# Third layer of a four-layer graph network: attention matrix and transformed rows split into rounded parts, their float32 product written as three rounded products

## The reference, cut to what matters

```python
h = jnp.maximum(_layernorm(x, axis=-1), 0.0)
Wh = jnp.einsum('bni,hoi->bhno', h, W) + bW[None, :, None, :]
e = jnp.einsum('bhno,hop->bhnp', Wh, attn)
scores = jnp.einsum('bhnp,bhmp->bhnm', e, Wh)
A_mat = jnp.tanh(jnp.where(adj[:, None, :, :], scores, 0.0))
```

## Time and profile before

| | |
|---|---|
| median of 3 runs | 2121.08 us (2115.74, 2121.08, 2121.89) |
| the profiled execution | 2115.82 us |
| its span, first to last instruction | 2113.7 us |
| mean granted TensorE clock | 0.991 |
| busy: PE (matmul) / PEld (weight load) | 2029.5 us (96%) / 1882.4 us (89%) |
| busy: DVE, ACT, POOL | 1488.5, 1001.3, 572.5 us (70%, 47%, 27%) |
| third layer's steps | about 753 to 1640 us of the span |

### The profile page before, as it was taken

The page is one execution under the profiler, slowest core; times in us unless marked ns, Lnnn a source line. Parts: engine busy times, 40 slices in busy tenths (PEclk is TensorE's granted clock), DMA queues, the critical chain, the costliest instruction groups (busy, mean ns, idle before and its releaser), DMA issues. The chain is left out here.

```text
span 2113.7 us, 52824 instructions
## 1 busy us (share of the span) xinstructions
PE 2029.5 (96%) x18448; PEld 1882.4 (89%) x18448; DVE 1488.5 (70%) x3344; ACT 1001.3 (47%) x2058; POOL 572.5 (27%) x624
## 2 busy tenths in 40 slices
PE   7999999899999799999999999999998899999997
PEld 7888888899999699999999999999998788888886
DVE  7989989677777455555555555555555699999997
ACT  6666666455555322232222322322222476767665
POOL 4444434222222011101111111011111444454443
PEclk9999999999999899999999999999999999999999
DMA  3222222532323201011111110111110112221221
GB/s 107 68 75 76 65 71 76 153 90 80 91 76 91 74 16 28 21 31 30 30 30 30 30 30 16 30 30 30 30 30 21 38 52 61 61 61 49 57 61 46
DMA packets 149370, 113.31 MB, mean 54 GB/s; under 512 B 42944, under 2 KB 148800, under 8 KB 149312
## 3 DMA queue, kind: packets, MB, share of 16 engines
q1 hardware_dynamic: 149312, 112.52, 18.8%
HBM read 78.93 MB, written 33.55 MB: 53 GB/s over the span
## 5 line engine op out<-in xcount | busy, mean ns | idle before, releaser
L254 POOL TENSOR_TENSOR ln_rstd<-ln_var_eps,minus_half 128x2 f32<-128x2 f32 x128 | 95.4, 745 | 888.1 <-DVE ln_var_eps L247 888.1
L1703 ACT ACTIVATE l_cat_hi<-banks 128x512 fp32r<-128x512 f32 x128 | 76.5, 598 | 261.3 <-PE banks L1874 261.3
L271 ACT ACTIVATE ln_h<-ln_x,ln_shift,ln_rstd 128x256 f32<-128x256 f32 x256 | 139.5, 592 | 57.5 <-DVE ln_shift L261 51.9
L162 PE MATMUL banks<-ln_hT_hi,square_w_hi 128*128 128x256 f32 x512 | 154.3, 301 | 5.0 <-DVE square_w_lo L628 3.2
L162 PE MATMUL banks<-ln_hT_hi,l_g_w_hi 128*128 128x256 f32 x512 | 148.5, 290 | 4.1 <-PEq L1972 4.1
L164 PE MATMUL banks<-ln_hT_hi,square_w_lo 128*128 128x256 f32 x512 | 145.7, 285 | 0.0
L163 PE MATMUL banks<-ln_hT_lo,square_w_hi 128*128 128x256 f32 x512 | 145.7, 284 | 0.0
L162 PE MATMUL banks<-l_cat_hi,l_aw_hi 128*128 128x256 f32 x512 | 144.2, 282 | 1.4 <-DVE l_cat_lo L1761 1.4
L164 PE MATMUL banks<-l_cat_hi,l_aw_lo 128*128 128x256 f32 x512 | 144.1, 281 | 0.0
L163 PE MATMUL banks<-l_cat_lo,l_aw_hi 128*128 128x256 f32 x512 | 143.9, 281 | 0.0
L164 PE MATMUL banks<-ln_hT_hi,l_g_w_lo 128*128 128x256 f32 x512 | 142.7, 279 | 0.0
(11 more groups left out here) (237 smaller groups left out, 6946.4 us busy)
## 6 DMA issues: line engine op xcount, KB each, us to landing
hidden<-y SPq DMA_DIRECT2D x96, 256.0 KB, 2.2
ln_x<-hidden SPq DMA_DIRECT2D x96, 256.0 KB, 2.8
x_res<-hidden SPq DMA_DIRECT2D x96, 256.0 KB, 3.0
ln_x<-x SPq DMA_DIRECT2D x32, 256.0 KB, 2.9
x_res<-x SPq DMA_DIRECT2D x32, 256.0 KB, 3.0
out<-y SPq DMA_DIRECT2D x32, 256.0 KB, 2.2
l_adj_u<-adj SPq DMA_DIRECT2D x96, 16.0 KB, 2.4
l_stage_attnT<-L_attnT SPq DMA_DIRECT2D x4, 256.0 KB, 3.2
```

The costliest lines, as they stand in the source:

```text
L162: nc.tensor.matmul(out, lhs(lh), rhs(rh), start=start, stop=False, skip_group_check=True)
L254: self.nc.gpsimd.tensor_tensor(self.rstd[:, g.slot], self.var_eps[:, g.slot], self.core.minus_half[:, 0:PAIRS], ALU.pow).then_inc(self.rst ...
L271: last = self.nc.scalar.activation(self.h[:, u, p, :], self.x[:, u, p, :], ACT.Relu, bias=self.shift[:, u, p:p + 1], scale=self.rstd[:, u, ...
L1703: nc.scalar.activation(cat_hi[:, h * KC:(h + 1) * KC], halves(B_HP[h]), ACT.Relu).then_inc(cat_hi_ready.sem, 1)
```

## The change

- `a_bd` becomes two rounded tensors, `a_hi` and `a_lo`, `wh` gets `wh_hi` and `wh_lo`, and `product_hp` calls `mm3`: per group 48 rounded matmuls in place of 16 float32 ones.
- The mask is now multiplied into `th` in place, by the same two engines. ScalarE then copies `th` to `a_hi` (two ACTIVATEs, partitions 0 to 63 and 64 to 127). GpSimd subtracts for the lower half of `a_lo`, right behind its mask product. VectorE subtracts for the upper half, and does so behind the evacuations of `g` 0 and 1 and ahead of those of `g` 2 and 3.
- ScalarE copies `wh` to `wh_hi` (two ACTIVATEs of 1024 columns), between `ln.apply` and `c_diag_hi`; GpSimd subtracts for `wh_lo` (two of 1024 columns), behind `c_diag`.
- TensorE's product of head 0 waits for `a_lo` of both engines and for `wh_lo`.
- For room, `wh` is put over a weight staging area that is no longer read, and `part` and `yT` over `diff`, worked in place; the wait for the transposes of the blend before moves ahead of the first of the three.

```diff
-                    after(pool, hp_in_psum, c2.back(1))
-                    nc.gpsimd.tensor_tensor(a_bd[0:S, :, :, 0, :], th[0:S],
+                    nc.gpsimd.tensor_tensor(th[0:S], th[0:S],
                                             adj[0:S, c2.slot].unsqueeze(2).to_broadcast([S, PAIRS, H, S]),
                                             ALU.mult).then_inc(a_pool_ready.sem, 1)
+                    after(pool, a_hi_ready, c2, 1)
+                    after(pool, hp_in_psum, c2.back(1))
+                    nc.gpsimd.tensor_tensor(a_lo[0:S, :, :, 0, :], th[0:S], a_hi[0:S, :, :, 0, :],
+                                            ALU.subtract).then_inc(a_lo_pool_ready.sem, 1)
...
+                    after(pool, hp_in_psum, b1.back(1))
+                    for p in range(PAIRS):
+                        after(pool, wh_hi_ready, b1, p + 1)
+                        nc.gpsimd.tensor_tensor(wh_lo[:, p], wh[:, p, 0:H * D], wh_hi[:, p],
+                                                ALU.subtract).then_inc(wh_lo_ready.sem, 1)
...
+                    after(act, a_pool_ready, c2)
+                    nc.scalar.activation(a_hi[0:S, :, :, 0, :], th[0:S], ACT.Copy).then_inc(a_hi_ready.sem, 1)
+                    after(act, a_dve_ready, c2)
+                    nc.scalar.activation(a_hi[S:P, :, :, 1, :], th[S:P], ACT.Copy).then_inc(a_hi_ready.sem, 1)
...
+                    after(act, wh_ready, b1, 3)
+                    nc.scalar.activation(wh_hi[:, 0], wh[:, 0, 0:H * D], ACT.Copy).then_inc(wh_hi_ready.sem, 1)
+                    after(act, wh_ready, b1)
+                    nc.scalar.activation(wh_hi[:, 1], wh[:, 1, 0:H * D], ACT.Copy).then_inc(wh_hi_ready.sem, 1)
...
+                if c2.exists(groups):
+                    after(dve, a_hi_ready, c2)
                     after(dve, hp_in_psum, c2.back(1))
...
+                    nc.vector.tensor_tensor(a_lo[S:P, :, :, 1, :], th[S:P], a_hi[S:P, :, :, 1, :],
+                                            ALU.subtract).then_inc(a_lo_dve_ready.sem, 1)
...
-                            last = nc.tensor.matmul(ps[:, B_HP[h], col:col + P],
-                                                    wh[:, p, h * D + c * P:h * D + (c + 1) * P],
-                                                    a_bd[:, p, h].rearrange("q b t -> q (b t)"), start=True, stop=True)
+                            f0 = h * D + c * P
+                            last = mm3(nc, ps[:, B_HP[h], col:col + P], (wh_hi, wh_lo), (a_hi, a_lo), True, True,
+                                       lambda w: w[:, p, f0:f0 + P],
+                                       lambda m: m[:, p, h].rearrange("q b t -> q (b t)"))
...
-                    after(pe, a_pool_ready, c2)
-                    after(pe, a_dve_ready, c2)
-                    after(pe, wh_ready, c2)
+                    after(pe, a_lo_pool_ready, c2)
+                    after(pe, a_lo_dve_ready, c2)
+                    after(pe, wh_lo_ready, c2)
```

More of the change, by code:

```diff
@@ L1584, in graph_attention_layer @@
         gT = sb("gT", [P, H, KC, TOK])
-        wh = sb("wh", [P, PAIRS, WC])
+        wh = (next_weights.square.raw[:].rearrange("p a c d -> p (a c d)")[:, 0:PAIRS * WC]
+              .rearrange("p (q n) -> p q n", q=PAIRS))
+        wh_hi, wh_lo = [sb(n, [P, PAIRS, H * D], F32R) for n in ("wh_hi", "wh_lo")]
         c_diag = sb("c_diag", [P, PAIRS, H, S])
@@ L1588, in graph_attention_layer @@
         th = sb("th", [P, PAIRS, H, S])
-        a_bd = sb("a_bd", [P, PAIRS, H, 2, S])
+        a_hi, a_lo = [sb(n, [P, PAIRS, H, 2, S], F32R) for n in ("a_hi", "a_lo")]
         cat_hi, cat_lo = sb("cat_hi", [P, CH, TOK], F32R), sb("cat_lo", [P, CH, TOK], F32R)
@@ L1595, in graph_attention_layer @@
         diff = sb("diff", [P, KC, TOK])
-        part = sb("part", [P, KC, TOK])
-        yT = sb("yT", [P, KC, TOK])
+        part = yT = diff
         x_res, y = core.x_res, core.y
@@ L1655, in _ @@
         def _(pool):
-            nc.gpsimd.memset(a_bd[:], 0.0).then_inc(zeroed.sem, 1)
-            pool.wait_ge(zeroed.sem, 1)
+            nc.gpsimd.memset(a_hi[:].bitcast(F32), 0.0).then_inc(zeroed.sem, 1)
+            nc.gpsimd.memset(a_lo[:].bitcast(F32), 0.0).then_inc(zeroed.sem, 1)
+            pool.wait_ge(zeroed.sem, 2)
             def step(g):
@@ L1694, in step @@
                     after(act, scores_in_psum, c2)
-                    after(act, a_pool_ready, c2.back(1))
-                    after(act, a_dve_ready, c2.back(1))
+                    after(act, a_lo_pool_ready, c2.back(1))
+                    after(act, a_lo_dve_ready, c2.back(1))
                     nc.scalar.activation(th[:], ps[:, B_S, :].rearrange("p (q h t) -> p q h t", q=PAIRS, h=H),
                                          ACT.Tanh).then_inc(th_ready.sem, 1)
+                    after(act, hp_in_psum, c2.back(1))
+                    if c2.reg is None and c2.c == 0:
+                        act.wait_ge(zeroed.sem, 2)
+                    after(act, a_pool_ready, c2)
+                    nc.scalar.activation(a_hi[0:S, :, :, 0, :], th[0:S], ACT.Copy).then_inc(a_hi_ready.sem, 1)
+                    after(act, a_dve_ready, c2)
+                    nc.scalar.activation(a_hi[S:P, :, :, 1, :], th[S:P], ACT.Copy).then_inc(a_hi_ready.sem, 1)
                 if c2.exists(groups):
@@ L1707, in step @@
                 if b1.exists(groups):
+                    after(act, hp_in_psum, b1.back(1))
+                    after(act, wh_lo_ready, b1.back(1))
+                    after(act, wh_ready, b1, 3)
+                    nc.scalar.activation(wh_hi[:, 0], wh[:, 0, 0:H * D], ACT.Copy).then_inc(wh_hi_ready.sem, 1)
+                    after(act, wh_ready, b1)
+                    nc.scalar.activation(wh_hi[:, 1], wh[:, 1, 0:H * D], ACT.Copy).then_inc(wh_hi_ready.sem, 1)
                     after(act, c_diag_ready, b1)
@@ L1751, in evacuate_wh @@
                     if i == 0:
-                        after(dve, hp_in_psum, b1.back(1))
+                        after(dve, wh_hi_ready, b1.back(1))
+                        after(dve, wh_lo_ready, b1.back(1))
                         after(dve, c_diag_ready, b1.back(1))
@@ L1767, in step @@
                     after(dve, gate_ready, e)
+                    after(dve, yT_in_psum, e.back(1))
                     nc.vector.tensor_tensor(diff[:], hf[:, e.slot], halves(B_HA), ALU.subtract).then_inc(blend_steps.sem, 1)
@@ L1772, in step @@
                     after(dve, blend_steps, e, 2)
-                    after(dve, yT_in_psum, e.back(1))
                     nc.vector.scalar_tensor_tensor(out=yT[:], in0=part[:], scalar=0.5, in1=halves(B_HA), op0=ALU.mult,
@@ L1781, in step @@
                     after(dve, adj_ready, c2)
[L1782 to L1785, removed]
+                    nc.vector.tensor_tensor(th[S:P], th[S:P],
                                             adj[S:P, c2.slot].unsqueeze(2).to_broadcast([S, PAIRS, H, S]),
@@ L1792, in step @@
                     evacuate_g(1)
+                if c2.exists(groups):
+                    after(dve, a_hi_ready, c2)
+                    after(dve, hp_in_psum, c2.back(1))
+                    if c2.reg is None and c2.c == 0:
+                        dve.wait_ge(zeroed.sem, 2)
+                    nc.vector.tensor_tensor(a_lo[S:P, :, :, 1, :], th[S:P], a_hi[S:P, :, :, 1, :],
+                                            ALU.subtract).then_inc(a_lo_dve_ready.sem, 1)
                 if e.exists(groups):
```

5 lines of the change are left out of this document (4 added, 1 removed).

## The result

The changed kernel takes 2316.5 us in the median of four runs (2288.9 to 2319.0), the kernel before 2121.5. The ratio is **1.090** (95% interval 1.084 to 1.097): slower by 9%, where I had forecast 4% and a range up to 2250 us. The profiled execution took 2318.96 us, 203 us more than that of before.

What follows compares the result with a forecast made beforehand. TensorE was taken to bound the kernel (matmuls busy 96% of the span). 2115.8 us plus 57.5 for products and 30 for the wait gave 2203; half of the runs' 5.3 us offset made it 2206 us, range 2158 to 2250.

Steps and rivals of the forecast that it cites:

- The product: Third layer's product_hp on TensorE: 24 rounded matmuls at 112 ns replace 8 float32 ones per two heads, +57.5 us.
- low bound of 64 by columns: Rounded product if columns alone set the pace: 64 ns each, -16 us; with the wait 2130 us, chance 0.09.
- The dear rival: Rounded matmuls of 128 columns go at the float32 price of 224 ns: +229 us, 2375 us in all; chance 0.07.
- The 81 ns of the Trainium skill: Pairs of load and matmul at 128 columns take about 81 ns, making the product term +10 us instead.
- The rule of passes: Float32 is four passes, three rounded products three: 1.34 us for two heads, -29 us; stands beside the faster case, chance 0.04.
- The way to head 0: New TensorE wait ahead of head 0 for a_lo, GpSimd last: 0.93 us a group, +30 us for 32.
- The bound of 1.5 us: Upper bound of the wait ahead of head 0, if each of three semaphores costs 0.2 us more: +48 us.
- granted clock of 1.00: TensorE's clock in the third layer before the change (2.4 GHz), read from the profile.
- Costed at nothing: Late evacuations of g 2 and 3, wh_hi copies, wh_lo subtractions (5.2 us on GpSimd), moved blend wait, one memset: no cost.

Runs made afterwards that it cites:

- e6: e3 with 64 moving columns instead of 128 in each of the 48 rounded products, half of the output left out: 2242.3 us, ratio 1.059.
- e7: e3 with 64 columns of weights instead of 128 in each of the 48 rounded products, half of the features left out: 2109.6 us, ratio 0.997.
- e5: e3 with a_hi, a_lo, wh_hi and wh_lo in bfloat16 instead of the rounded 4-byte type, a coarser split: 2101.3 us, ratio 0.992.
- e3: Changed kernel, full computation, with product_wh 0 and 1 ahead of heads 0 and 1 on TensorE and some VectorE evacuations moved earlier: 2189.0 us, ratio 1.034.
- e2: Changed kernel with its waits and splits kept but the float32 product put back, a_lo left out of the result: 2179.5 us, ratio 1.030.
- e4: Changed kernel with both halves of a_lo made by VectorE, GpSimd's subtraction taken out: 2234.0 us, ratio 1.055.
- e1: Changed kernel with the 48 products reading hT_hi and hT_lo, so TensorE does not wait for a_lo: 2200.4 us, ratio 1.039.
- e9: Changed kernel in its own order, wait kept, with the four split tensors in bfloat16: 2150.9 us, ratio 1.015.

## Why the prediction was wrong

**The product: right.** I took 112 ns a rounded product, the price of the load, against a low bound of 64 by columns. At full clock it measured 112 to 113, and e6, e7 and e5 show that it is the load. The term was +1.80 us a step; e3 has +1.93. The rest is most likely a pause ahead of the next matmul that I had counted to the float32 product alone. The dear rival (224 ns) is not what the 213 ns in the trace are: those come only at a clock of 0.50. The 81 ns of the Trainium skill ("TensorE: Matmul & The Clock Gate", section Back-to-back issue gap) fits neither type here, 112 and 57. The rule of passes of the Trainium skill ("FP8 and Floating Point Precision", TensorE Precision Notes), three for four, leaves loads out. With the cheap loads of e5 it comes out: 24 x 57 ns = 1.37 us against 1.79, 0.76; with those of the rounded type it does not, 2.69 against 1.79.

**The way to head 0: the right chain, the size half.** I had 0.93 us a group, 30 us; the trace has 1.7 and e2 shows (1682.8 - 754.4)/31 - 28.12 = 1.83 us a step for it, its product being the float32 one:

```profile
L1710 ACT ACTIVATE l_th<-banks x32: 597/602/602, 754.4 to 1682.8; 128x512 f32<-128x512 f32 x32
```

What was missing is that VectorE and GpSimd would subtract out of SBUF at the same time. I priced VectorE's 0.69 us from rows in which GpSimd was idle or VectorE read PSUM, and called GpSimd the last; in the step above VectorE ends 0.56 us behind GpSimd. I had also given ScalarE's second copy 0.49 us (1180.16 to 1180.65) where its own row has 0.63; it took 0.63, and with that the forecast's own rows have the two engines level. The bound of 1.5 us was too low as well. e4, without the sharing, gets 17 us of the waits back; what makes up the rest of the difference was not taken apart.

**The failed step: the "granted clock of 1.00" was taken to stay.** My sum priced all of TensorE's work at full clock and had no rival in which the clock falls. Behind 1.7 us of idle and with load-bound products it was 0.91 in the layer instead. Of the step's 6.03 us more, 1.93 are products and 1.83 the wait; 2.27 us are left, 70 us over 31 steps. This remainder is what the two changes cost together over what each costs alone, and the falls of the clock, which e1, e2 and e9 take away, are what goes with it. The layer's clock row bounds it from above: 0.09 x 1087 us = 98 us, some of it time that was idle anyway. The medians say the same: e2 costs 62 us over before and e3 71, together 133, but both at once cost 195, 62 more. By this the time without the falls would have been some 2317 - 62 = 2255 us, an estimate: still at the edge of the range, since the wait was twice its forecast size.

**Costed at nothing: held, with one exception.** The `wh` splits cost TensorE nothing (GpSimd's 5.2 us as forecast), nor do the late evacuations as long as TensorE is late itself. In e1, where it is not, VectorE's late `a_lo` costs 14 us by `cat_lo`; in the changed kernel the wait for `a_lo` covers that.

What stays open: why in some steps of the changed kernel the clock falls and in others not, and why e4, with 1.1 us of idle, has some falls left. Neither was tried further.

## What to carry to other kernels

Price a matmul by the larger of its columns and its weight load, each from a row: with 128x128 weights of 4 bytes, splitting one float32 product of 128 columns into three buys three loads of 112 ns for two. With parts of 2 bytes it paid 16 us here, for a coarser result. With 256 moving columns it should pay; that is an estimate, 3 x 119 = 357 ns against 2 x 256 x 0.82 = 420 ns for float32, and no run here shows it. Ask of every new idle on TensorE what stands behind it: ahead of load-bound products, 0.6 us of it more (1.7 in place of 1.1 a group) took the layer's clock from 0.98 to 0.91, ahead of products that stream it cost about its own length (e9: 50 us of idle, 50 us more than e5; e2: 53 us of idle, 62 us over the kernel before). And when a chain is short by a microsecond, look first for work that can stand ahead of the waiting instruction: here it gave back 124 of 195 us.

## What the runs showed of the hardware that I had not expected

- The granted clock fell with PE busy 100% of the time (e6): there the busy share did not show it coming.
- Loads of 128x128 weights last 190 ns in the rounded 4-byte type and 100 ns in bfloat16; matmuls of 128 columns come every 112 and every 57 ns.
- Two engines out of SBUF at once: VectorE's split of `c_diag`, beside GpSimd's new `wh_lo`, went from 0.69 to 2.21 us. TensorE was busy with other products meanwhile and waited for it once, 3.4 us in the first group (1.9 us before):

```profile
L1816 DVE TENSOR_TENSOR l_c_diag_lo<-l_c_diag,l_c_diag_hi x32: 692/693/693, 748.1 to 1614.6; 128x512 fp32r<-128x512 f32 x32
```

```profile
L1847 DVE TENSOR_TENSOR l_c_diag_lo<-l_c_diag,l_c_diag_hi x32: 2152/2208/2217, 751.4 to 1807.0; 128x512 fp32r<-128x512 f32 x32
```

The first is the kernel before, the second the changed one.
